# Which engine empties the output bank in a causal attention loop: VectorE or ScalarE

## What is computed

```
h = rmsnorm(x, ln1_w)
qkv = einsum('bsh,oh->bso', h, wqkv)          # 16 query heads, 4 key/value heads, 16 wide
q, k = rope(q), rope(k);  k, v repeated 4 times over the heads
scores = einsum('bqhd,bkhd->bhqk', q, k) * 16 ** -0.5
scores = where(tril, scores, min);  probs = softmax(scores)
attn = einsum('bhqk,bkhd->bqhd', probs, v)
x = x + attn @ wo.T                            # then a top-2 of 8 experts layer
```

## Time and profile before

| | us |
|---|---|
| three runs | 1739.2, 1738.49, 2075.5 |
| their median | 1739.2 |
| the profiled execution's own time | 1730.77 |
| its span, first to last instruction | 1729.1 |
| mean granted clock of TensorE | 0.968 |
| the attention steps, in the span | about 353 to 1212 |

### The profile page before, as it was taken

How to read it: one execution, slowest core, us unless ns; L and a number is a source line. 1 busy time by engine, 2 the same in 40 slices (tenths; PEclk the granted TensorE clock), 3 DMA queues, 4 the chain that set the end, 5 groups by cost and what they waited for, 6 DMA issues and landing times. The chain is left out here.

```text
span 1729.1 us, 29571 instructions
## 1 busy us (share of the span) xinstructions
PE 1624.7 (94%) x9040; PEld 807.7 (47%) x9040; DVE 1166.1 (67%) x3195; ACT 931.3 (54%) x2069; POOL 556.0 (32%) x842
## 2 busy tenths in 40 slices
PE   7899989899999999999999999998995899999996
PEld 3367655333333333334333343332884455565554
DVE  6722788899888888888888888870685344343342
ACT  6134544166676776676676766667573333333332
POOL 3530338163515003030030300000377344444443
PEclk9999999799999999999999999999895899999999
DMA  5000000311030300303003030000378677777774
GB/s 165 1 7 19 2 1 7 62 36 28 2 62 2 62 2 1 62 2 62 2 1 62 2 62 2 1 1 1 120 234 276 122 129 130 131 130 129 129 126 71
DMA packets 252195, 105.77 MB, mean 61 GB/s; under 512 B 208064, under 2 KB 247880, under 8 KB 252040
## 3 DMA queue, kind: packets, MB, share of 16 engines
q1 hardware_dynamic: 233296, 80.62, 22.0%
q0 software_dynamic: 13392, 18.49, 6.3%
q10 hardware_dynamic: 5352, 4.76, 0.8%
HBM read 30.88 MB, written 23.67 MB: 32 GB/s over the span
## 5 line engine op out<-in xcount | busy, mean ns | idle before, releaser
L1677 ACT ACTIVATE prob<-pS 128x512 f32<-128x512 f32 (+3 forms) x1280 | 582.3, 542 | 267.5 <-PE pS L1563 176.2
L1734 DVE TENSOR_REDUCE mx<-pM 128x1 f32<-128x512 f32 x768 | 501.6, 685 | 71.3 <-PE pM L1543 68.1
L1543 PE MATMUL pM<-KT,QT 96*128 96x512 bf16 (+3 forms) x1280 | 434.1, 356 | 16.5 <-DVE mx L1734 5.5
L1559 PE MATMUL pS<-QT,KT 99*128 99x512 bf16 (+3 forms) x1280 | 422.9, 352 | 6.8 <-ACT prob L1677 1.8
L2440 PE MATMUL bank<-w13T,QKV 128*128 x568 | 257.2, 596 | 15.4 <-ACT QKV L2467 15.4
L1730 DVE CUSTOM_DVE_ANT_0 junk<-pM,mask_row 128x128 bf16<-128x128 f32 (+3 forms) x512 | 239.9, 483 | 41.7 <-PE pM L1543 41.1
L1578 PE MATMUL pO<-prob,VV 128*32 128x512 f32 (+3 forms) x2560 | 267.8, 536 | 0.0
L1543 PEld LDWEIGHTS pM<-KT,QT 96*128 96x128 bf16 x1280 | 124.5, 98 | 208.5 <-DVE mx L1734 79.1
L1468 POOL CAST mpart<-mneg 128x16 bf16<-128x16 f32 x32 | 6.8, 213 | 653.9 <-DVE mneg L1742 653.9
L1559 PEld LDWEIGHTS pS<-QT,KT 99*128 99x128 bf16 x1280 | 123.6, 97 | 184.0 <-ACT prob L1677 140.2
L2500 DVE TENSOR_TENSOR QKV<-QKV,bank 128x512 f32<-128x512 f32 x71 | 48.8, 687 | 235.5 <-issue 200.2
(11 more groups left out here) (356 smaller groups left out, 1947.3 us busy)
## 6 DMA issues: line engine op xcount, KB each, us to landing
raw<-in_ffn_w_dram SPq DMA_DIRECT2D x48, 256.0 KB, 4.0
QKV<-queue SPq DMA_DIRECT2D x71, 136.0 KB, 2.5
out_dram<-x ACTq DMA_DIRECT2D x8, 512.0 KB, 4.7
x<-_attn_hidden_states_dram SPq DMA_DIRECT2D x14, 256.0 KB, 5.5
QKV<-QKV SPq DMA_TRANSPOSE x142, 3.2
QT<-mrow SPq DMA_DIRECT2D x128, 3.0 KB
out_dram<-QKV POOLq DMA_INDIRECT x71, 3.9
wc_s<-in_attn_Wc_dram SPq DMA_DIRECT2D x1, 1024.0 KB, 8.1
```

Of the source, the lines that this page charges most:

```text
L1543: last = nc.tensor.matmul(pM[:, bank, 0:w], QT[0:ROWS, par, h, qt * P:(qt + 1) * P], KT[0:ROWS, par, 512 * part:512 * part + w], start=Tru ...
L1559: last = nc.tensor.matmul(pS[:, p % NSC, lo:512], KT[0:ROWS + 3, par, kt * P:(kt + 1) * P], QT[0:ROWS + 3, par, h, 512 * c + lo:512 * c + ...
L1677: nc.scalar.activation(prob[:, n % RING, h, lo:512], pS[:, p % NSC, lo:512], ACT.Exp, scale=SCALE).then_inc(s.head_exp, 1)
L1734: nc.vector.reduce_max(mx[:, h, qt, part:part + 1], pM[:, plan.bank[item], 0:w], AX.X).then_inc(s.unit_max, 1)
```

## The change

The copy of `pO` to `oS` moves from VectorE to ScalarE. In VectorE's list it stood behind the units of the step in which the values product finishes. In ScalarE's list it stands at the end of that same step, that is behind the exponential of the fourth head of the next step. It waits for the same two semaphores. VectorE gets one more wait ahead of its reciprocal (for its own earlier product, `o_put`), since the copy no longer stands between them. TensorE's, GpSimd's and SyncE's lists do not change.

```
@block.scalar
+                def chunk(k, n):
+                    act.wait_ge(s.pv, n)
+                    if k:
+                        act.wait_ge(s.o_mm, k)
+                    nc.scalar.copy(oS[:, :], pO[:, :]).then_inc(s.o_out, 1)
...
                 for n in range(len(STEPS)):
...
                         if n + 1 < len(STEPS) and head is not None:
                             exponential(n + 1, head)
+                    gi, c, kt = STEPS[n]
+                    if n and kt == 0:
+                        chunk(CH * gi + c - 1, n)
+                chunk(CH * NG - 1, len(STEPS))
@block.vector
-                def chunk(k, n):
-                    dve.wait_ge(s.pv, n)
-                    if k:
-                        dve.wait_ge(s.o_mm, k)
-                    nc.vector.tensor_copy(oS[:, :], pO[:, :]).then_inc(s.o_out, 1)
-
                 def chunk_put(k):
                     gi, c = k // CH, k % CH
                     t0, g = gi // NKV * TB, gi % NKV
                     dve.wait_ge(s.o_mm, k + 1)
+                    if k:
+                        dve.wait_ge(s.o_put, k)
...
-                    if n and kt == 0:
-                        chunk(CH * gi + c - 1, n)
-                chunk(CH * NG - 1, len(STEPS))
                 chunk_put(CH * NG - 1)
```

## The result

| | median, us | runs | ratio to the kernel before | 95% interval |
|---|---|---|---|---|
| before | 1738.5 | 7 | | |
| changed | 1745.0 | 7 | 1.0035 | 1.0023 to 1.0048 |
| changed, second measurement | 1743.8 | 7 | 1.0043 | 1.0029 to 1.0057 |

The change makes the kernel slower by 0.35%, 6 us (4 to 8), clear of noise and well inside the 2%. The forecast was 1746.8 us, +7.6. One of the seven runs of the kernel before took 2075.5 us, and the ratios leave it out. The second measurement has its own runs of the kernel before, with a median of 1737.3 us.

A forecast was written before the change was run, and what follows sets the result against it. ScalarE's exponentials, through the ring of three score banks, were taken to set the pace. Terms 3.84 + 2.31 + 1.32 + 1.38 - 1.0 - 0.3 = +7.6 us on 1739.2 gave 1746.8 us, range 1733 to 1758.

The forecast's parts named there:

- What bounds the kernel: Behind chunk 2, scores start as soon as ScalarE frees one of three score banks, slack 0.05 us; ScalarE sets the pace.
- The slot: On ScalarE, each added copy takes a slot of 0.48 us in the run of exponentials, bounds 0.47 and 0.60.
- The price of each place: Slot less the tightest score's slack: 0.48, 0.33, 0.22, 0.23 us behind chunks 2, 3, 0, 1.
- The turn of `oS` is not delayed by the copy itself: Tightest behind chunk 3: copy over at about 578.03, turn starts at 578.22, so the copy adds no delay.
- a sign that its theory is wrong: In the profile after, TensorE seen idle before the transposes of L1587 would show the theory wrong.
- VectorE's relief: Counts only where TensorE waits for maxima: -1.0 us in the first group, -0.3 us in the last.
- The sum: Over all places, the costs less the gains come to +7.6 us, giving 1746.8 us, 0.4% slower.
- The hidden copy: Rival: ScalarE gives the slot back in its 1.86 us idle; only -1.3 us remains, 1737.9 us; chance 0.22.
- The relief of VectorE: Rival: VectorE was tighter and its relief wins, 1733.7 us, or 1720.6 if it paced every place; chance 0.15.
- The rival of the turn: The turn of `oS` becomes TensorE's new wait, over 2% slower, needing 1.1 us at each of 31 places; chance 0.02.

The follow-up runs named there:

- experiment 1: Changed kernel with the ScalarE copy moved two exponentials forward, in front of the first exponential behind the values product: 1734.8 us, ratio 1.000 to the kernel before.
- experiment 6: Changed kernel with four score banks and three unit banks in place of three and four: 1755.2 us, ratio 1.0107 to the kernel before.
- experiment 2: Changed kernel with a second 512-column copy on ScalarE right behind the first, into a buffer nobody reads: 1760.6 us, ratio 1.0149 to the kernel before.
- Experiment 4: Changed kernel with the turn of oS and the next unit swapping pM banks behind chunk 0 of groups 2 to 7: 1747.7 us, ratio 1.0069.
- experiment 3: Changed kernel with a stand-in maximum over 512 constant columns on VectorE where the old copy stood: 1743.7 us, ratio 1.0047 to the kernel before.
- experiment 7: Kernel of experiment 1 with the copy back on VectorE behind chunk 2 (8 places): 1735.4 us, ratio 0.9987 to the kernel before.
- experiment 5: Kernel before, copy on VectorE, with four score banks and three unit banks in place of three and four: 1766.0 us, ratio 1.0155.
- experiment 9: Kernel of experiment 7 measured once more, unchanged: 1735.2 us, ratio 0.9982 to the kernel before.

## Why the prediction was right, and where it was not

- **What bounds the kernel: right.** The ring of three score banks, refilled by ScalarE, sets the pace in the run of eight exponentials. The profile after shows it (a slot in, a slot lost, the idle time at the cycle's end unchanged), and experiments 1 and 6 tell it from load: behind chunk 2 the same copy costs 0.13 us at another position and, in most groups, nothing with a fourth bank. A middle group grew by 1.39 us for 1.26 forecast.
- **The slot: right.** 0.47 us at 0.48 forecast, 580 ns long at 580. By the Trainium skill ("ScalarE: Activation LUTs", "What ACT_TABLE_LOAD costs") the estimate was 0.52 us. The trace has 0.47 to 0.48 behind exponentials from PSUM. The second copy of experiment 2, which reads SBUF, did take 0.52.
- **The price of each place: right at chunk 2, 0.05 and 0.06 us too high at chunks 3 and 1, too low at chunk 0.** Behind chunks 3 and 1 the slack of the score was read rightly (it came 0.34 and 0.25 us later, for 0.33 and 0.23), but the place had also waited a little for VectorE, and that wait went away: 0.28 and 0.17 us were left. For chunk 3 the rows above show it; for chunk 1 I take it from the 0.09 us that the place gains in experiment 1. The row of chunk 3 in the table agrees (2.30 for 2.31) only because one of its places took 0.56 us and one 0.36, which is luck. Why these two took more I leave open. Behind chunk 0 the term was mis-sized, 0.22 for 0.47 us each, 1.5 us in all. The step that failed is "The turn of `oS` is not delayed by the copy itself": I tested that for the turn's operand and at the tightest place, and not for the bank it writes. Experiment 4 shows the bank as the cause of 0.23 of the 0.25 us. TensorE is idle for 0.13 us ahead of L1587 there (484.62 to 484.75), which the prediction had named as a sign that its theory is wrong; at these six places it was.
- **VectorE's relief: right in kind, a little small.** It counts at the places where TensorE waits for maxima, and experiment 3 shows that in the changed kernel it counts nowhere else. With the copy early on ScalarE (experiments 1 and 7) the places behind chunks 1 and 3 gain 0.09 and 0.07 us as well. It was worth the whole 0.60 us at the second place, where I took only the 0.41 of one waiting row; a second row of 0.21 us stood behind it. At the last group's first place it was 0.52 for 0.28, at its second 0.09 for 0.
- **The sum: +7.6 forecast, +8.3 in the places, +6.1 (4.0 to 8.3) in the medians.** The +1.5 us missed behind chunk 0 and the -0.9 us missed behind chunk 1 and in the first and last group have opposite signs, so the sum is closer than its terms, which is luck.
- **The rivals.** The hidden copy falls: experiment 2 shows slots paid in full, and the idle 1.86 us took nothing in. The relief of VectorE does not win here. It wins as soon as the unit ring is the tight one, as experiments 5 and 6 show; the Trainium skill's advice ("TensorEngine Tiling (Array Packing)", "PSUM Bottleneck") to use both engines for emptying PSUM is then borne out at 0.5 to 0.6%, and here only once the copy stands where ScalarE idles (experiments 7 and 9). The rival of the turn was seen in small: by its bank, at six of the 31 places, for 0.25 us and not for the 1.1 that it would have needed.

## What to carry to other kernels

An engine that is busy for 70% can set the pace, and one that is busy for 87% may have room: read at the very place which wait ends last, and how much slack the ring of buffers has there. Before an instruction is moved to an engine with more air, look for the place in that engine's list where it idles. Behind chunk 2 the same copy cost 0.47 us in a run of exponentials and 0.13 us two exponentials earlier. And for each instruction that now stands behind the moved one, ask also whose buffer it frees.

## What was not expected of the hardware

TensorE's granted clock fell to its lower level for some 3 us in the first attention group of three of the traces with three score banks, and not in the others, which did nearly the same work; it cost 1.4 to 1.6 us each time. Executions of one and the same kernel also differed by 4.5 us in when the attention steps began (348.5 and 353.1 us, at a mean granted clock of 0.94 and 0.93 up to there). The pattern inside the loop repeated to 0.02 us at nearly every place, so a change of 0.1 us per place can be read there while the whole span moves by several us.
